# Softmax denominators inverted in PSUM, row maxima dealt over pairs of steps, and five more probability tiles a unit summed on GpSimd

## The chip, the cores and the metric

The kernel runs on one core of one Trainium2 chip. The metric is the device time of one execution in microseconds (us).

## The reference

A transformer block on x of shape (4, 2048, 512): an adaptive layernorm (shift, scale and gate from a small product), causal attention with 16 heads of 32 channels, and a feedforward of the RWKV kind. The change touches the attention alone. All is float32.

```python
scores = jnp.einsum('bqhd,bkhd->bhqk', q, k)
scores = scores + jnp.einsum('bqr,bkr->bqk', q_rope, k_rope)[:, None]
scores = scores / scale
causal = jnp.triu(jnp.ones((Tt, Tt), dtype=bool), k=1)
scores = jnp.where(causal[None, None], -jnp.inf, scores)
w = jax.nn.softmax(scores, axis=-1)
attn = jnp.einsum('bhqk,bkhd->bqhd', w, v).reshape(Bb, Tt, D_MODEL)
return attn @ W_o
```

## The kernel before

The program has three stages: the projection (to about 510 us), the attention (to about 3034 us) and the feedforward. The attention works through 16 units; a unit u is four heads of one batch entry. A unit has four groups j = 0 to 3 of 512 queries each. Group j goes over the 128-key tiles that its queries may see: 4(j+1) steps, 40 in a unit. In the last four steps of a group the diagonal cuts the columns to 512, 384, 256 and 128 (`step_width`), and GpSimd zeroes the triangle with an `affine_select` (L915). FIRST = 0, 4, 12, 24 are the first steps of the groups; here steps are numbered within the unit, and those behind 39 are the next unit's.

What a step t makes on each engine:

- TensorE: for each of four heads two matmuls of scores into one of three banks (L985, L986). In every odd step the output products of steps t-3 and t-2 follow (`weighted_values`, eight instructions a step, into ps_o).
- ScalarE: four exponentials into one of five probability tiles (`probs`, RING = 5, L831).
- The denominators: the sum of the probabilities over all keys. SHARE_OF names the owner of each step. On a "T" step TensorE multiplies the probabilities with ones into ps_d beside the output product. The "G" steps are added by GpSimd into `sum_g` (L934 for the first two, L937 for the others), and one product with ones, the closing (`close_denominators`), brings `sum_g` into ps_d, at step 1 of the next group. Before, group 0 has no G step and no closing.
- VectorE, behind a closing: a copy of ps_d to `rden` (L878), four reciprocals of 128 columns in `rden` (L884), and the product of the output (`o_sb`, which ScalarE copied from ps_o) with `rden` (L888, the normalisation), spread over the two steps behind the closing (`extras`).
- The row maxima: 160 pieces a unit, each a score matmul of 128 queries by up to 512 keys into one of three banks (L971) and a maximum out of the bank on VectorE (L867, or L870 with the mask where the keys are those of the diagonal). A piece is named by its group j and its key chunk kc; those with kc < j are full (512 columns), those with kc = j are 128, 256, 384 or 512 wide. When a group's pieces are done, TensorE transposes the maxima (the "turn", L959), VectorE negates them (L861), and a DMA puts them into a row of the score operand. PLAN says between which score matmuls the pieces stand, for work that is due up to 30 steps later. TensorE and VectorE take the pieces in one order, and TensorE may be three pieces ahead.

The order on each engine is written out in full by the program; nothing is rearranged when it runs. `denominators_ready`, `den_taken` and `o_ready` are semaphores between TensorE and VectorE, `cleared` and `sum_added` come from GpSimd. The output product of a step waits for `cleared` when the step is one of the last four of its group.

Of the kernel before, what the change touches and what calls it, by code (L numbers as in the profile page):

```python
# [22 lines left out]
P = 128  # L23
# [521 lines left out]
SHARE_OF = ("TTTT", "GGGGTGGG", "GGGTGGGGTGGG", "GGGTGGGTGGGGTGGG")  # L545
# [8 lines left out]
def sum_shares():  # L554

    out = []
    for j, owners in enumerate(SHARE_OF):
        mine = [i for i, o in enumerate(owners) if o == "G"]
        if mine:
            out += [(j, (mine[0], mine[1]))] + [(j, (i,)) for i in mine[2:]]  # L560
    return out
# [7 lines left out]
def room(s):  # L569

    if s == NSTEP:
        return CH // 2
    return step_width(s) * (2 if any(s - FIRST[j] in (2, 3) for j in range(1, TCH)) else 5) // 5


def maximum_plan():

    plan = {t: [] for t in range(NU * NSTEP)}
    early = lambda it: it[-1] == 0
    spans = []  # L580
    for u in range(NU):
        mine = [[(u, *it) for it in max_pieces(j)] for j in range(TCH)]
        if u == 0:
            spans += [(u, mine[1], range(0, 3)), (u, mine[2], range(3, 11)), (u, mine[3], range(11, 22))]
        else:
            spans += [(u - 1, mine[0] + [it for it in mine[2] if early(it)] + mine[1], range(23, NSTEP + 1)),
                      (u, [it for it in mine[2] if not early(it)] + mine[3], range(2, 22))]
    for u, items, steps in spans:
        seen, done = 0, 0
        for s in steps:  # L590
            seen += room(s)
            upto = len(items) * seen // sum(map(room, steps))
            plan[NSTEP * u + s] += items[done:upto]
            done = upto
# [52 lines left out]
def attention(nc, keep, scratch, ops):  # L647


    with ExitStack() as ctx:  # L650
# [15 lines left out]
        rden, *o_sb = (sb(n, [P, CH], F32) for n in ("rden", "o_sb0", "o_sb1"))  # L666
# [13 lines left out]
        den_ready = sem("den_ready")  # L680
        den_taken, rden_ready = sem("den_taken"), sem("rden_ready")
# [21 lines left out]
        SHARES = sum_shares()  # L703
# [9 lines left out]
        def summed(u, j, i):  # L713

            return len(SHARES) * (u + 1) + next(n for n, (jj, steps) in enumerate(SHARES) if jj == j and i in steps) + 1

        CLOSED = [j for j in range(TCH) if set(SHARE_OF[j]) != {"T"}]

        def denominators_ready(u, j):

            if j not in CLOSED:
                return pv_done, NSTEP * u + FIRST[j] + STEPS[j] + RING
            return den_ready, len(CLOSED) * u + CLOSED.index(j) + 2
# [811 lines left out]
```

## Time and profile before

| | us |
|---|---|
| three runs | 3919.67 median (3917.86 to 3922.95) |
| the profiled execution | 3919.98 |
| its span in the trace | 3918.3 |
| TensorE busy | 3643.2 (93%) |
| VectorE busy | 2844.3 (73%) |
| GpSimd busy | 2444.0 (62%) |
| ScalarE busy | 1805.1 (46%) |

Busy times are sums of instruction times over the span. The end of a matmul is modelled, so two matmuls in a row overlap; the distance from one start to the next is the time that one takes in the stream. A wait is the idle time of an engine, put down to the instruction that ended it.

### The profile page before, as it was taken

Reading aid. Unit: us, or ns where it says so; the run is one execution under the profiler, and the core shown is the slowest. Engines: PE = TensorE matmul, PEld = TensorE weight load, DVE = VectorE, ACT = ScalarE, POOL = GpSimd, SP = SyncE. Lnnn points to the kernel's source line nnn. Section 1 sums busy time; section 2 is a strip of 40 time slices with the busy share of each in tenths; the row PEclk is TensorE's granted clock in tenths of the full one; section 3 lists DMA queues with packets and bytes.
Section 4 is the critical chain, followed back from the end, with each engine's and each line's share of the span. In section 5 each row is a group of like instructions: output and inputs, shape, how many; then the busy total and the mean of one; then the engine's idle time right before and its main releaser. Section 6 shows DMA issues by size and latency. Waiting matters only on the chain. (4 is left out here: it accounts for less than half of the span.)

```text
span 3918.3 us, 56697 instructions
## 1 busy us (share of the span) xinstructions
PE 3643.2 (93%) x19808; PEld 2454.7 (63%) x19808; DVE 2844.3 (73%) x5454; ACT 1805.1 (46%) x3401; POOL 2444.0 (62%) x1145
## 2 busy tenths in 40 slices
PE   7999879999999999999999999999998699999998
PEld 3777645665665665656656666566564577777776
DVE  5777577777777777778777777777773577777776
ACT  2343335555555555555555555555554233333332
POOL 1333237677777787777777867777778355555555
PEclk8999989999999999999999999999999799999999
DMA  5789743463543634634436345344430311111110
GB/s 176 258 270 296 264 99 76 90 134 78 113 98 83 141 79 95 135 73 108 104 88 130 79 103 127 76 106 109 90 83 6 129 64 54 64 57 53 61 64 32
DMA packets 232267, 425.83 MB, mean 109 GB/s; under 512 B 25332, under 2 KB 26868, under 8 KB 231928
## 3 DMA queue, kind: packets, MB, share of 16 engines
q1 hardware_dynamic: 231992, 423.10, 41.5%
q8 instruction: 121, 1.98, 0.2%
q14 instruction: 90, 0.74, 0.1%
q10 hardware_dynamic: 64, 0.02, 0.0%
HBM read 300.86 MB, written 121.65 MB: 108 GB/s over the span
## 5 line engine op out<-in xcount | busy, mean ns | idle before, releaser
L831 ACT ACTIVATE att_probs<-att_ps_s 128x512 f32<-128x512 f32 (+3 forms) x2560 | 1316.4, 534 | 1153.9 <-PE att_ps_s L986 1058.3
L937 POOL TENSOR_TENSOR att_sum_g<-att_sum_g,att_probs 128x2048 f32<-128x2048 f32 (+3 forms) x384 | 1447.3, 3769 | 207.3 <-ACT att_probs L831 171.6
L867 DVE TENSOR_REDUCE att_piece_max<-att_ps_m 128x1 f32<-128x512 f32 x1536 | 973.1, 680 | 218.6 <-PE att_ps_m L971 215.6
L985 PE MATMUL att_ps_s<-att_q_a,att_k_a 128*128 128x512 f32 (+3 forms) x2560 | 962.2, 380 | 15.8 <-DMA att_q_b<-att_neg_max 15.7
L986 PE MATMUL att_ps_s<-att_q_b,att_k_b 65*128 65x512 f32 (+3 forms) x2560 | 942.5, 371 | 0.0
L971 PE MATMUL att_ps_m<-att_k_a,att_q_a 128*128 128x512 f32 (+3 forms) x1840 | 674.3, 391 | 72.6 <-DVE att_piece_max L867 36.1
L870 DVE CUSTOM_DVE_ANT_0 att_ps_m<-att_ps_m,mask_qk 128x128 f32<-128x128 f32 (+3 forms) x1024 | 489.5, 507 | 291.4 <-PE att_ps_m L971 281.0
L985 PEld LDWEIGHTS att_ps_s<-att_q_a,att_k_a 128*128 128x128 f32 x2560 | 491.5, 192 | 137.1 <-issue 61.6
L971 PEld LDWEIGHTS att_ps_m<-att_k_a,att_q_a 128*128 128x128 f32 x1840 | 348.2, 192 | 350.1 <-DVE att_piece_max L867 129.1
L992 PE MATMUL att_ps_o<-att_probs,att_v 128*32 128x512 f32 (+3 forms) x5120 | 549.4, 535 | 7.3 <-POOL att_probs L915 7.3
L986 PEld LDWEIGHTS att_ps_s<-att_q_b,att_k_b 65*128 65x128 f32 x2560 | 489.2, 191 | 68.0
L934 POOL TENSOR_TENSOR att_sum_g<-att_probs 128x2048 f32<-128x2048 f32 x48 | 221.3, 4610 | 389.5 <-PE att_ps_d L992 217.6
L971 PE MATMUL att_ps_m<-att_k_next,att_q_a 128*128 128x128 f32 (+1 forms) x720 | 275.9, 390 | 32.2 <-DVE att_piece_max L870 32.2
L992 PEld LDWEIGHTS att_ps_o<-att_probs,att_v 128*32 128x32 f32 x5120 | 133.5, 109 | 250.7 <-issue 162.9
L915 POOL TENSOR_SCALAR_AFFINE_SELECT att_probs<-att_probs 128x512 f32<-128x512 f32 x256 | 161.6, 634 | 114.7 <-ACT att_probs L831 114.7
L884 DVE RECIPROCAL att_rden<-att_rden 128x128 f32<-128x128 f32 x256 | 232.5, 930 | 0.1
L971 PEld LDWEIGHTS att_ps_m<-att_k_next,att_q_a 128*128 128x128 f32 x720 | 140.5, 195 | 120.8 <-issue 47.1
L1379 POOL TENSOR_TENSOR ffn_x_kept<-ffn_x_kept,ffn_gate_r 128x512 f32<-128x512 f32 x64 | 101.6, 1588 | 163.6 <-DVE ffn_gate_r L1256 163.6
L1172 DVE TENSOR_TENSOR ffn_x<-ffn_ps_ffn,ffn_gate 128x512 f32<-128x512 f32 x64 | 44.3, 692 | 169.8 <-PE ffn_ps_ffn L61 142.5
L1322 ACT ACTIVATE ffn_act_f<-ffn_relu 128x512 f32<-128x512 f32 x64 | 40.4, 632 | 257.1 <-DVE ffn_relu L1251 256.2
L888 DVE TENSOR_TENSOR att_o_sb<-att_o_sb,att_rden 128x512 f32<-128x512 f32 x64 | 153.5, 2399 | 1.1
L59 PE MATMUL ffn_ps_ffn<-ffn_w_o_hi,ffn_att_hi 128*128 128x512 f32 x256 | 108.5, 424 | 43.9 <-ACT ffn_gate_r L1316 38.5
(173 smaller groups left out, 5230.1 us busy)
## 6 DMA issues: line engine op xcount, KB each, us to landing
att_q_a<-s_q_hi SPq DMA_DIRECT2D x128, 256.0 KB, 6.4
att_q_a<-s_qr_hi SPq DMA_DIRECT2D x128, 256.0 KB, 7.2
prj_x_sb<-in_x_dram SPq DMA_DIRECT2D x16, 1024.0 KB, 5.4
s_q_hi<-prj_q_hi SPq DMA_DIRECT2D x16, 1024.0 KB, 4.4
s_q_lo<-prj_q_lo SPq DMA_DIRECT2D x16, 1024.0 KB, 6.5
s_k_hi<-prj_k_hi SPq DMA_DIRECT2D x16, 1024.0 KB, 4.5
s_k_lo<-prj_k_lo SPq DMA_DIRECT2D x16, 1024.0 KB, 6.5
s_v<-prj_v_sb SPq DMA_DIRECT2D x16, 1024.0 KB, 9.4
```

The lines of the kernel that those rows point to most:

```text
L831: act.activation(probs[t % RING][:, hh, c0:CH], ps_s[(GH * t + hh) % SBANKS][:, c0:CH], ACT.Exp, scale=SCALE).then_inc(probs_ready, 1)
L867: dve.tensor_reduce(top, ps_m[:, bank, :], AX_X, ALU.max).then_inc(piece_taken, 1)
L870: dve.tensor_tensor_reduce(ps_m[:, bank, 0:width], ps_m[:, bank, 0:width], keep["mask_qk"][:, CH - width:CH], 1.0, MASKED, ALU.add, ALU.ma ...
L884: dve.reciprocal(cols, cols).then_inc(rden_ready, 1)
L888: dve.tensor_tensor(o_sb[j % 2][:], o_sb[j % 2][:], rden[:], ALU.mult).then_inc(o_ready, 1)
L915: pool.affine_select(out=at, in_=at, compare_op=ALU.is_ge, fill=0.0, base=0, pattern=[[0, GH], [1, P]], channel_multiplier=-1).then_inc(cl ...
L934: pool.tensor_tensor(sum_g[:], probs[(FIRST[j] + steps[0]) % RING][:], new, ALU.add).then_inc(sum_added, 1)
L937: pool.tensor_tensor(sum_g[:, :, c0:CH], sum_g[:, :, c0:CH], new, ALU.add).then_inc(sum_added, 1)
L971: mm(ps_m[:, bank, 0:width], q_a[j][:, hh, r * P:(r + 1) * P], keys, start=True, stop=True).then_inc(piece_ready, 1)
L985: mm(out[:, c0:CH], k_a[:, hh, i * P:(i + 1) * P], q_a[j][:, hh, c0:CH], start=True, stop=False)
L986: last = mm(out[:, c0:CH], k_b[:, hh, i * P:(i + 1) * P], q_b[j][:, hh, c0:CH], start=False, stop=True)
L992: last = mm(out[hh * HD:(hh + 1) * HD, c0:CH], stat(hh), mov[:, hh, c0:CH], start=start, stop=stop, skip_group_check=True)
```

## The change

The reciprocals are taken in ps_d, in place, and the normalisation reads ps_d; `rden` and its copy are gone. So ps_d is free for the next group only when the normalisation is done: where TensorE waited for `den_taken` it waits for `o_ready`.

SHARE_OF gives GpSimd 35 steps a unit where it had 30, and TensorE five where it had ten. Group 0 is now summed by GpSimd in its first two steps: a copy of 128 columns of each head and an addition of 384 (`head`), and so it has a closing as well, in step 5, ahead of the output products of steps 2 and 3, whose T products come behind it. On GpSimd the head stands between the clearing of steps 0 and 1 and that of steps 2 and 3, and it waits for the closing of the group before (`closed`). Group 1 has no T step left: its closing opens ps_d.

The plan of the maxima is new: `deal` hands them out over pairs of steps. A pair gets as many as make the ratio of VectorE's work to TensorE's the same in every pair, with 2.8 for a piece and 19 for the denominators of a group that fall into the pair. The order of the groups' pieces changes too, and pieces are dealt from step 24 of the unit before to step 21.

```diff
--- before.py
+++ after.py
@@ -542,7 +542,7 @@
 
 
 LAG = 2
-SHARE_OF = ("TTTT", "GGGGTGGG", "GGGTGGGGTGGG", "GGGTGGGTGGGGTGGG")
+SHARE_OF = ("GGTT", "GGGGGGGG", "GGGGGGGGTGGG", "GGGGGGTGGGGGTGGG")
 
 
 def step_width(s):
@@ -551,47 +551,71 @@
     return CH - max(0, s - FIRST[j] - TB * j) * P
 
 
-def sum_shares():
-
-    out = []
+def sums_made():
+
+    made, read_by = [], {}
     for j, owners in enumerate(SHARE_OF):
         mine = [i for i, o in enumerate(owners) if o == "G"]
-        if mine:
-            out += [(j, (mine[0], mine[1]))] + [(j, (i,)) for i in mine[2:]]
+        if j == 0:
+            made.append((j, "head"))
+        for n, i in enumerate(mine):
+            if n:
+                made.append((j, i))
+            read_by[j, i] = len(made) + (n == 0)
+    return made, read_by
+
+
+def max_pieces(j):
+
+    return [(j, hh, r, kc) for kc in range(j + 1) for hh in range(GH) for r in range(TB)]
+
+
+def streams(m):
+
+    own = sum(2 * GH * step_width(s) for s in (2 * m, 2 * m + 1))
+    due = [(2 * m - 2) % NSTEP, (2 * m - 1) % NSTEP]
+    for s in due:
+        j = max(j for j in range(TCH) if FIRST[j] <= s)
+        own += GH * step_width(s) * (2 if SHARE_OF[j][s - FIRST[j]] == "T" else 1)
+    return own / CH + GH * any(FIRST[j] == (2 * m) % NSTEP for j in range(TCH))
+
+
+PIECE, CLOSING = 2.8, 19
+
+
+def deal(items, pairs):
+
+    closes = lambda m: CLOSING * any(FIRST[j] + 2 == 2 * m for j in range(TCH))
+    share = lambda rho, m: max(0.0, (rho * streams(m) - closes(m)) / (PIECE - rho))
+    low, high = 0.0, PIECE - 0.01
+    for _ in range(60):
+        rho = (low + high) / 2
+        low, high = (rho, high) if sum(share(rho, m % (NSTEP // 2)) for m in pairs) < len(items) else (low, rho)
+    out, seen = {}, 0.0
+    for m in pairs:
+        for half in (0, 1):
+            done = round(seen)
+            seen += share(high, m % (NSTEP // 2)) / 2
+            out[2 * m + half] = items[done:round(seen)]
+    assert sum(map(len, out.values())) == len(items)
     return out
 
 
...
 def maximum_plan():
 
-    plan = {t: [] for t in range(NU * NSTEP)}
...
+    half = NSTEP // 2
     for u in range(NU):
...
+        part = {(j, kc): [(u, *it) for it in max_pieces(j) if it[-1] == kc] for j in range(TCH) for kc in range(j + 1)}
         if u == 0:
...
+            spans = [(part[1, 0] + part[1, 1], range(0, 1)), (part[2, 0] + part[2, 1] + part[2, 2], range(2, 5)),
+                     (sum((part[3, kc] for kc in range(TCH)), []), range(5, 11))]
         else:
...
+            order = ((0, 0), (1, 0), (2, 0), (1, 1), (2, 1), (2, 2), (3, 0), (3, 1), (3, 2), (3, 3))
+            spans = [(sum((part[p] for p in order), []), range(half * u - half + 12, half * u + 11))]
+        for items, pairs in spans:
+            for t, some in deal(items, pairs).items():
+                plan[t] += some
...
-        rden, *o_sb = (sb(n, [P, CH], F32) for n in ("rden", "o_sb0", "o_sb1"))
+        o_sb = [sb(n, [P, CH], F32) for n in ("o_sb0", "o_sb1")]
...
@@ -700,7 +724,7 @@
 
...
-        SHARES = sum_shares()
+        MADE, READ_BY = sums_made()
 
         def heads_ready(u, s, hh):
 
@@ -712,15 +736,13 @@
 
         def summed(u, j, i):
 
-            return len(SHARES) * (u + 1) + next(n for n, (jj, steps) in enumerate(SHARES) if jj == j and i in steps) + 1
-
-        CLOSED = [j for j in range(TCH) if set(SHARE_OF[j]) != {"T"}]
+            return len(MADE) * (u + 1) + READ_BY[j, i]
 
         def denominators_ready(u, j):
 
-            if j not in CLOSED:
+            if j == 0:
                 return pv_done, NSTEP * u + FIRST[j] + STEPS[j] + RING
-            return den_ready, len(CLOSED) * u + CLOSED.index(j) + 2
+            return closed, TCH * u + j + 2
 
 
         STEP_OF = [(u, j, i) for u in range(NU) for j in range(TCH) for i in range(STEPS[j])]
@@ -850,7 +872,6 @@
         def _(dve):
             dve.sem_inc(o_ready, 1)
             dve.sem_inc(rden_ready, TB)
-            dve.sem_inc(den_taken, 1)
 
             def maxima(items):
 
@@ -873,23 +894,18 @@
                         dve.wait_ge(piece_taken, seq + 1)
                         dve.tensor_reduce(row_max[:, j, :], piece_max[:, j, :, 0:j + 1], AX_X, ALU.max).then_inc(max_ready, 1)
 
-            def take_denominators(u, j):
-                waits(dve, denominators_ready(u, j), (o_ready, TCH * u + j + 1))
-                dve.tensor_copy(rden[:], ps_d[:]).then_inc(den_taken, 1)
-
             def invert(u, j, r):
                 if r == 0:
-                    dve.wait_ge(den_taken, TCH * u + j + 2)
-                cols = rden[:, r * P:(r + 1) * P]
+                    dve.wait_ge(*denominators_ready(u, j))
+                cols = ps_d[:, r * P:(r + 1) * P]
                 dve.reciprocal(cols, cols).then_inc(rden_ready, 1)
 
             def normalise(u, j):
                 waits(dve, (rden_ready, TB * (TCH * u + j + 2)), (o_copied, TCH * u + j + 2))
-                dve.tensor_tensor(o_sb[j % 2][:], o_sb[j % 2][:], rden[:], ALU.mult).then_inc(o_ready, 1)
+                dve.tensor_tensor(o_sb[j % 2][:], o_sb[j % 2][:], ps_d[:], ALU.mult).then_inc(o_ready, 1)
 
             extras = {t: [] for t in range(NU * NSTEP + LAG + 2)}
             for t, (u, j) in CLOSE_AT.items():
-                extras[t + 1].append(lambda u=u, j=j: take_denominators(u, j))
                 for r in range(TB):
                     extras[t + 1 + r // 2].append(lambda u=u, j=j, r=r: invert(u, j, r))
                 extras[t + 2].append(lambda u=u, j=j: normalise(u, j))
@@ -903,11 +919,9 @@
 
         @block.gpsimd
         def _(pool):
-            pool.sem_inc(sum_added, len(SHARES))
-            pool.sem_inc(den_ready, 1)
+            pool.sem_inc(sum_added, len(MADE))
+            pool.sem_inc(closed, 1)
             pool.memset(as_f32(k_b[2 * HD:2 * HD + 1, :, :]), 1.0).then_inc(ones_ready, 1)
-
-            shares = {(j, steps[-1]): steps for j, steps in SHARES}
 
             def clear_future(u, j, i):
 
@@ -921,18 +935,24 @@
                         s = FIRST[j] + i
                         c0 = CH - step_width(s)
                         new = probs[s % RING][:, :, c0:CH]
-                        steps = shares.get((j, i), ())
-                        if i < TB * j and steps:
+                        mine = [n for n, o in enumerate(SHARE_OF[j]) if o == "G"]
+                        makes = i in mine[1:]
+                        if i < TB * j and makes:
                             pool.wait_ge(probs_ready, heads_ready(u, s, GH - 1))
                         if i >= TB * j:
                             wait_alone(pool, probs_ready, heads_ready(u, s, GH - 1), pool_mark)
                             clear_future(u, j, i)
-                            if steps:
+                            if makes:
                                 pool.wait_ge(cleared, future_cleared(u, j, i))
-                        if len(steps) == 2:
-                            pool.wait_ge(den_ready, len(CLOSED) * u + CLOSED.index(j) + 1)
-                            pool.tensor_tensor(sum_g[:], probs[(FIRST[j] + steps[0]) % RING][:], new, ALU.add).then_inc(sum_added, 1)
-                        elif steps:
+                        if not makes:
+                            continue
+                        if i == mine[1]:
+                            first = probs[(FIRST[j] + mine[0]) % RING]
+                            pool.wait_ge(closed, TCH * u + j + 1)
+                            if c0:
+                                pool.tensor_copy(sum_g[:, :, 0:c0], first[:, :, 0:c0]).then_inc(sum_added, 1)
+                            pool.tensor_tensor(sum_g[:, :, c0:CH], first[:, :, c0:CH], new, ALU.add).then_inc(sum_added, 1)
+                        else:
                             pool.wait_ge(sum_added, summed(u, j, i) - 1)
                             pool.tensor_tensor(sum_g[:, :, c0:CH], sum_g[:, :, c0:CH], new, ALU.add).then_inc(sum_added, 1)
 
@@ -1010,25 +1030,28 @@
                 last = over_keys(ps_o, lambda hh: v[:, i // TB, i % TB, hh * HD:(hh + 1) * HD], probs[s % RING],
                                  start=(i == 0), stop=(i == STEPS[j] - 1), c0=c0)
                 if SHARE_OF[j][i] == "T":
-                    first = i == SHARE_OF[j].index("T")
+                    first = j > 0 and i == SHARE_OF[j].index("T")
                     if first:
-                        pe.wait_ge(den_taken, TCH * u + j + 1)
-                    last = over_keys(ps_d, ones, probs[s % RING], start=first,
-                                     stop=(j not in CLOSED and i == STEPS[j] - 1), c0=c0)
+                        pe.wait_ge(o_ready, TCH * u + j + 1)
+                    last = over_keys(ps_d, ones, probs[s % RING], start=first, stop=(j == 0 and i == STEPS[j] - 1), c0=c0)
                 last.then_inc(pv_done, 1)
 
             def close_denominators(u, j):
-                if "T" not in SHARE_OF[j]:
-                    pe.wait_ge(den_taken, TCH * u + j + 1)
+                opens = j == 0 or "T" not in SHARE_OF[j]
+                if opens:
+                    pe.wait_ge(o_ready, TCH * u + j + 1)
                 pe.wait_ge(sum_added, summed(u, j, SHARE_OF[j].rindex("G")))
-                last = over_keys(ps_d, ones, sum_g, start=("T" not in SHARE_OF[j]), stop=True)
-                last.then_inc(den_ready, 1)
+                last = over_keys(ps_d, ones, sum_g, start=opens, stop=(j > 0))
+                last.then_inc(closed, 1)
 
             for item in AHEAD:
                 maximum(item)
             pe.wait_ge(ones_ready, 1)
             for t in range(NU * NSTEP + LAG):
                 parts = [lambda hh=hh: scores(*STEP_OF[t], hh) for hh in range(GH) if t < NU * NSTEP]
+                closing = CLOSE_AT.get(t)
+                if closing and closing[1] == 0:
+                    parts.append(lambda: close_denominators(*closing))
                 if t > LAG and t % 2 == 1:
                     parts.append(lambda: [weighted_values(*STEP_OF[due]) for due in (t - LAG - 1, t - LAG)])
                 items = PLAN.get(t, [])
@@ -1036,8 +1059,8 @@
                     part()
                     for it in items[len(items) * n // len(parts):len(items) * (n + 1) // len(parts)]:
                         maximum(it)
-                if t in CLOSE_AT and CLOSE_AT[t][1] in CLOSED:
-                    close_denominators(*CLOSE_AT[t])
+                if closing and closing[1] > 0:
+                    close_denominators(*closing)
 
 
 def feedforward(nc, keep, dram, scratch, out):
```

## Rows read from the trace of the kernel before

**Rows 1.** Waits of TensorE in the attention, 541 to 3034 us.
```profile
PE att_ps_m L971 <- DVE att_piece_max L870: 51.7, 35, 2.2
PE att_ps_m L971 <- DVE att_piece_max L867: 35.7, 18, 4.2
```
**Rows 2.** Timeline of TensorE: start, length, instruction, [idle before it <- releaser].
```profile
912.39 0.50 PE L971 MATMUL att_ps_m<-att_k_a,att_q_a 128*128 128x512 f32 x1 [1.93 <-DVE att_piece_max L867]
...
1222.24 0.50 PE L971 MATMUL att_ps_m<-att_k_a,att_q_a 128*128 128x512 f32 x1 [1.96 <-DVE att_piece_max L867]
...
1272.32 0.50 PE L971 MATMUL att_ps_m<-att_k_next,att_q_a 128*128 128x512 f32 x1 [2.13 <-DVE att_piece_max L870]
...
1347.68 0.39 PE L971 MATMUL att_ps_m<-att_k_a,att_q_a 128*128 128x256 f32 x1 [1.26 <-DVE att_piece_max L870]
...
2937.84 0.50 PE L971 MATMUL att_ps_m<-att_k_a,att_q_a 128*128 128x512 f32 x1 [1.93 <-DVE att_piece_max L867]
```
**Rows 3.** Windows, PE alone: us, PE busy, PE clock granted, DMA share, GB/s.
```profile
1220.00:1230.00 10.00, 8.04 (x35) 0.83 0.08 28
```
**Rows 4.** Timeline of VectorE, two normalisations.
```profile
1219.14 2.45 DVE L888 TENSOR_TENSOR att_o_sb<-att_o_sb,att_rden 128x512 f32<-128x512 f32 x1
...
1267.85 4.14 DVE L888 TENSOR_TENSOR att_o_sb<-att_o_sb,att_rden 128x512 f32<-128x512 f32 x1
```
**Rows 5.** Timeline of GpSimd, the additions that ran at those times.
```profile
1216.46 4.57 POOL L937 TENSOR_TENSOR att_sum_g<-att_sum_g,att_probs 128x2048 f32<-128x2048 f32 x1
...
1266.89 4.54 POOL L937 TENSOR_TENSOR att_sum_g<-att_sum_g,att_probs 128x2048 f32<-128x2048 f32 x1
```
**Rows 6.** Tile att_rden, whole run: lengths in ns min/median/max, first and last start.
```profile
L884 DVE RECIPROCAL att_rden<-att_rden x256: 893/937/954, 545.2 to 3032.7; 128x128 f32<-128x128 f32 x128
L878 DVE COPY att_rden<-att_ps_d x64: 682/692/692, 544.0 to 3029.5; 128x512 f32<-128x512 f32 x64
L888 DVE TENSOR_TENSOR att_o_sb<-att_o_sb,att_rden x64: 691/2394/4660, 550.8 to 3033.6; 128x512 f32<-128x512 f32 x64
```
**Rows 7.** Tile ffn_ps_ffn, VectorE alone, 3100 to 3900 us.
```profile
L1172 DVE TENSOR_TENSOR ffn_x<-ffn_ps_ffn,ffn_gate x60: 691/692/693, 3114.0 to 3848.7; 128x512 f32<-128x512 f32 x60
```
**Rows 8.** Timeline of TensorE: four closings in a row, and one output product.
```profile
1322.17 1.06 PE L992 MATMUL att_ps_d<-att_sum_g,ones 128*32 128x512 f32 x8
...
1336.64 0.64 PE L992 MATMUL att_ps_o<-att_probs,att_v 128*32 128x256 f32 x8
...
1368.46 1.07 PE L992 MATMUL att_ps_d<-att_sum_g,ones 128*32 128x512 f32 x8
...
1416.95 1.06 PE L992 MATMUL att_ps_d<-att_sum_g,ones 128*32 128x512 f32 x8
...
1476.73 1.06 PE L992 MATMUL att_ps_d<-att_sum_g,ones 128*32 128x512 f32 x8
```
**Rows 9.** Timeline of TensorE: two scores, and the output products of two steps.
```profile
1208.22 0.40 PE L985 MATMUL att_ps_s<-att_q_a,att_k_a 128*128 128x512 f32 x1
1208.45 0.40 PE L986 MATMUL att_ps_s<-att_q_b,att_k_b 65*128 65x512 f32 x1
...
1216.55 1.92 PE L992 MATMUL att_ps_o<-att_probs,att_v 128*32 128x512 f32 x16
1218.40 0.50 PE L971 MATMUL att_ps_m<-att_k_a,att_q_a 128*128 128x512 f32 x1
```
**Rows 10.** Timeline of GpSimd: group 1 of a unit, first and last addition.
```profile
1337.19 4.61 POOL L934 TENSOR_TENSOR att_sum_g<-att_probs 128x2048 f32<-128x2048 f32 x1 [10.00 <-ACT att_probs L831]
...
1360.30 1.29 POOL L937 TENSOR_TENSOR att_sum_g<-att_sum_g,att_probs 128x512 f32<-128x512 f32 x1
```
**Rows 11.** The same in group 3 of the last unit.
```profile
2980.27 37.89 POOL L937 TENSOR_TENSOR att_sum_g<-att_sum_g,att_probs 128x2048 f32<-128x2048 f32 x8
```
**Rows 12.** Groups of instructions by form, 1000 to 2600 us: count | busy, mean ns | idle before.
```profile
L867 DVE TENSOR_REDUCE att_piece_max<-att_ps_m 128x1 f32<-128x512 f32 x977 | 619.6, 680 | 129.9 <-PE att_ps_m L971 127.9
...
L937 POOL TENSOR_TENSOR att_sum_g<-att_sum_g,att_probs 128x1536 f32<-128x1536 f32 x32 | 111.1, 3470 | 2.7
L915 POOL TENSOR_SCALAR_AFFINE_SELECT att_probs<-att_probs 128x512 f32<-128x512 f32 x168 | 106.1, 634 | 58.8 <-ACT att_probs L831 58.8
...
L937 POOL TENSOR_TENSOR att_sum_g<-att_sum_g,att_probs 128x512 f32<-128x512 f32 x31 | 39.9, 1287 | 2.6
```

More of the change, by code:

```diff
@@ L551, in step_width @@
     return CH - max(0, s - FIRST[j] - TB * j) * P
-def sum_shares():
-    out = []
+def sums_made():
+    made, read_by = [], {}
     for j, owners in enumerate(SHARE_OF):
         mine = [i for i, o in enumerate(owners) if o == "G"]
-        if mine:
-            out += [(j, (mine[0], mine[1]))] + [(j, (i,)) for i in mine[2:]]
-    return out
+        if j == 0:
[5 more added lines that the diff above has]
+    return made, read_by
@@ L564, in max_pieces @@
 def max_pieces(j):
     return [(j, hh, r, kc) for kc in range(j + 1) for hh in range(GH) for r in range(TB)]
[L569 to L573, printed above, removed]
+def streams(m):
[5 more added lines that the diff above has]
+    return own / CH + GH * any(FIRST[j] == (2 * m) % NSTEP for j in range(TCH))
@@ new lines @@
+PIECE, CLOSING = 2.8, 19
[13 more added lines that the diff above has]
+    assert sum(map(len, out.values())) == len(items)
+    return out
@@ L576, in maximum_plan @@
 def maximum_plan():
-    plan = {t: [] for t in range(NU * NSTEP)}
-    early = lambda it: it[-1] == 0
-    spans = []
+    plan = {t: [] for t in range(NU * NSTEP + 1)}
+    half = NSTEP // 2
     for u in range(NU):
-        mine = [[(u, *it) for it in max_pieces(j)] for j in range(TCH)]
+        part = {(j, kc): [(u, *it) for it in max_pieces(j) if it[-1] == kc] for j in range(TCH) for kc in range(j + 1)}
         if u == 0:
-            spans += [(u, mine[1], range(0, 3)), (u, mine[2], range(3, 11)), (u, mine[3], range(11, 22))]
-        else:
-            spans += [(u - 1, mine[0] + [it for it in mine[2] if early(it)] + mine[1], range(23, NSTEP + 1)),
-                      (u, [it for it in mine[2] if not early(it)] + mine[3], range(2, 22))]
@@ L588, in maximum_plan @@
[L588 to L594, printed above, removed]
+            spans = [(part[1, 0] + part[1, 1], range(0, 1)), (part[2, 0] + part[2, 1] + part[2, 2], range(2, 5)),
+                     (sum((part[3, kc] for kc in range(TCH)), []), range(5, 11))]
+        else:
+            order = ((0, 0), (1, 0), (2, 0), (1, 1), (2, 1), (2, 2), (3, 0), (3, 1), (3, 2), (3, 3))
+            spans = [(sum((part[p] for p in order), []), range(half * u - half + 12, half * u + 11))]
@@ L679, in attention @@
         o_copied = sem("o_copied")
-        den_ready = sem("den_ready")
-        den_taken, rden_ready = sem("den_taken"), sem("rden_ready")
+        closed = sem("closed")
+        rden_ready = sem("rden_ready")
         kn_in = sem("kn_in")
```

## The prediction

> **What bounds the kernel now.** I read the waits of TensorE first. Between 541 and 3034 us it idles in one place that repeats: in front of a score matmul for the maxima (L971), until VectorE has emptied a bank, 51.7 + 35.7 = 87.4 us in 53 waits [rows 1]. The timeline shows them as three a unit at fixed places, of 1.26, 1.96 and 2.13 us [rows 2]; everywhere else one matmul starts behind the other, 0.23 us apart [rows 9]. So TensorE's stream sets the time, and what a unit takes is its matmuls plus these waits. The first matmul behind the second kind of wait starts at 912.39 us in one unit and at 2937.84 us 13 units later [rows 2]: 155.8 us a unit. Four closings in a row divide a unit: 46.3 us from that of group 3 to that of group 1, 48.5 to that of group 2, 59.8 to the next of group 3 [rows 8]. Some waits also cost clock: in the ten us around the one at 1222 the granted clock is 0.83 [rows 3], so a third of them at 1.2 GHz instead of 2.4, about 1.7 us more. Not every unit has that: the stretches of rows 8 hold none and add up to 154.6, so the clock costs 1.2 us a unit on average.
>
> Why VectorE is late: the normalisation (L888) takes 0.69 to 4.66 us, median 2.39, for one and the same shape [rows 6]. The two of rows 4 end at 1221.59 and 1271.99, each 0.56 us behind the end of the GpSimd addition that ran meanwhile (1221.03 and 1271.43) [rows 4, 5]. It reads two operands in SBUF and waits until GpSimd is through; the maxima are queued behind it on VectorE, and TensorE waits for them once its three banks are full.
>
> **The change, part by part.**
>
> *The normalisation out of PSUM.* It keeps one operand in SBUF. The nearest row is L1172, a product of a PSUM and an SBUF tensor of the same size: 691 to 693 ns in all 60 cases, in a stage where GpSimd works too [rows 7]. I take 0.69 us; the other end is 2.4, no change. The copy of 0.69 us goes as well [rows 6]. Together VectorE is free 2.4 us earlier behind a closing, more than each of the three waits. The Trainium skill, SBUF — State Buffer, "Who interferes with whom", says that a VectorE instruction with two SBUF inputs contends with a GpSimd instruction that reads SBUF, and that one with at most one SBUF input does not. By that rule 0.69 is right; the trace agrees on the first half, and the second is what rows 7 suggest.
>
> *The reciprocals in PSUM.* No row has one there. From SBUF 128 columns take 937 ns [rows 6], far more than reading them can (a reduction reads 512 columns out of PSUM in 680 ns [rows 12]), so I take 0.94, with 0.9 and 2 times that, 1.9, as the ends. The Trainium skill speaks against the change here: VectorE: DVE Perf Modes, "The TRN2 errata", gives a VectorE instruction a fixed 120 cycles with a PSUM source and 58 from SBUF. By that, as an estimate, four reciprocals and the product take 0.3 us more; the copy out of PSUM and the free product out of SBUF in rows 6 show no such difference (0.69 both), and 0.3 us would be hidden. What hides this work is the plan: it deals 0, 1, 2 and 1 pieces to the pairs of steps behind the four closings, and TensorE needs 6 us for such a pair of full steps (16 score matmuls of 0.234 and two output products of 0.925 [rows 9], 5.6, and the pieces) against 4 x 0.94 + 0.69 = 4.45 us on VectorE. In the pair behind group 3's closing (256 and 128 columns) TensorE needs only about 3.7, but the next user of ps_d, the closing of group 0, comes 10 us later (below).
>
> *TensorE's denominators.* A full T step costs 0.925 us, since two steps of output products take 1.85 [rows 9]; one of 384 columns about 0.7. Removed are four full ones (group 0 step 0; group 1; one in group 2; one in group 3) and that of 384 columns: 4.4 us a unit. Added is one closing, 1.0 [rows 8].
>
> *The maxima moved.* A full piece costs TensorE 0.234 us, a masked one by its mean width 0.15 (an estimate from rows 9). Counting `maximum_plan` out, the three stretches have 52, 54 and 54 pieces before (16, 26 and 22 of them masked) and 40, 45 and 75 after (10, 27 and 27 masked). In place of 7 in a full step, which is 4.8 us of VectorE with 0.68 each [rows 12], there are mostly 5 or 6.
>
> *GpSimd.* It gets four full additions more a unit (one each in groups 1, 2 and 3; the fifth step goes into the head) of 37.89 / 8 = 4.74 us [rows 11], and the head: a copy of 512 columns and an addition of 1536. The copy isn't in the trace; 0.63 (one input) and 1.29 (two inputs) bound it, and I take 1.0; with 3.47 [rows 12] the head is 4.5 us. GpSimd cannot start on a group before the group before is closed. So each stretch has a chain of its own: closing (1.0), additions, next closing. TensorE's path is taken from the measured stretch.
>
> Group 0: from group 3's closing to the output product at 1336.64 are 14.5 us before [rows 8]. Less the T products (1.6) and 18 pieces for 12 (2.1), the closing of group 0 starts 10.8 us behind. GpSimd's head and two clearings (1.0 + 4.5 + 1.3) and VectorE's denominators (1.0 + 4.5) both fit, with 4 us over: no wait.
>
> Group 1: GpSimd took 1337.19 to 1361.59, 24.4 us [rows 10]; with one addition more 29.1. The stretch is 10.8 + 1.0 + 29.1 = **40.9**. TensorE alone would need 46.3 - 1.3 (wait) - 0.9 - 0.7 - 0.9 (T) + 1.0 - 2.3 (12 pieces less) = 41.2 at most, and 39.8 if the small waits inside the steps go too (my sum of its matmuls before is 43.6). So GpSimd ends last by about a us here.
>
> Group 2: three full additions more than group 1, 29.1 + 14.2 - 0.3 (a wait in rows 10's stretch) = 43.0, with the closing **44.0**. TensorE: 48.5 - 2.0 - 0.9 - 2.2 = 43.4 at most, 41.7 without small waits. GpSimd ends last again.
>
> Group 3: GpSimd 1.0 + 29.1 + 6 x 4.74 = 58.5. TensorE: 59.8 - 2.1 - 0.9 + 21 pieces more (4.5) = 61.3, and 1.1 for short waits at the dense pairs: **62.4**. TensorE is the bound, and here the change costs 2.6 us.
>
> A unit: 40.9 + 44.0 + 62.4 = 147.3, against 155.8: 8.5 less. That holds for units 1 to 14: 119 us. The first unit has a plan of its own, denser in its first four steps; I give it 3. In the last one there are no pieces behind step 21, and GpSimd bounds group 3 already now (eight additions back to back [rows 11]): -5.4 - 4.5 + 4.7 and the copy at the end -0.7, so 6 less. Sum: 119 + 3 + 6 = 128. The profiled execution took 3919.98, 0.3 above the median of the runs: **3792 us**.
>
> **The rivals.**
> *GpSimd's waits hurt more than they last.* For it: the chains of groups 1 and 2 are the bound by 1 to 2 us, TensorE then waits in front of an output product for `cleared`, and waits of 2 us have cost 1.7 us of clock in about a third of the cases [rows 3]; short waits in the stretches add up on GpSimd's chain too when the probabilities come late. Against: the waits are split in two and are each shorter than 1.96. Two lost clocks and 2 us of wait a unit are 5.4 us, 15 x 5.4 = 80: 3872 at worst, 3835 in the middle.
> *GpSimd keeps up.* If its additions start earlier than I count, TensorE's own 39.8 + 41.7 + 61.3 = 142.8 holds, 4.5 x 15 = 68 less: 3725. Against: the chain starts at a closing, and every link has a row.
> *The normalisation still waits* (2.4 us, not 0.69). Then VectorE needs 6.2 us in pairs of 6; with few pieces there this costs 1 us at three closings, 45 us: 3837.
> *Slower: the reciprocals are slow out of PSUM.* Each closing has about 6 us of cover, 1.3 us for each reciprocal. Beyond, four closings of four reciprocals pay 16 times the excess a unit, since the maxima and ps_d itself wait for them. It eats the 8.5 us at 1.3 + 0.53 = 1.85 us each, twice the row; at 2.5 us the time is 3792 + 15 x 19 = 4080. Against: a length that is 7 ns a column in SBUF is arithmetic and not access.
>
> **How the numbers follow.** The forecast, 3770 to 3815, has 0.50; GpSimd's waits or a late normalisation (3815 to 3872) 0.27; GpSimd keeps up (3725 to 3770) 0.13; a gain under 48 us that is still over 0.2% 0.03; none 0.02; slower 0.05. A measurement here tells 0.2% (8 us) from nothing. Range with two in ten outside: 3750 to 3850. Faster 0.93, same 0.02, slower 0.05.
>
> **What would show it.** Of the changed profile: L888 at 0.69 us throughout; the reciprocals at 0.94; no waits of L971 for VectorE above 1 us; new waits of TensorE for GpSimd in front of the output product of step 21 (about 2 us) and at the closing of group 1 (about 1); distances between closings of 41, 44 and 62; GpSimd without idle time from a closing of group 0 to that of group 2 but for the closings. It is wrong if L971 still waits for VectorE, if a closing waits for `o_ready`, or if the third stretch is shorter than 60.

## The result and the profile after

The changed kernel takes 3798.61 us (median of four runs, 3789.98 to 3807.10) against 3921.22 us for the kernel before (four runs, 3917.86 to 3922.95). The ratio is 0.9691, with a 95% interval from 0.9673 to 0.9708: 3.1% faster, 6.6 us from the 3792 that was predicted. The profiled execution took 3801.18 us, 118.8 less than that of before.

The page's busy times (first section, then the rows of the slices for TensorE and GpSimd):

```profile
PE 3586.7 (94%) x19296; PEld 2423.5 (64%) x19296; DVE 2702.1 (71%) x5390; ACT 1800.5 (47%) x3401; POOL 2722.6 (72%) x1225
...
PE   7999979999999999999999999999996899999998
...
POOL 1333248889889898898898898988986455555555
```

GpSimd is now eight or nine tenths busy throughout the attention; TensorE has 512 instructions fewer. The waits of TensorE in the attention, 541 to 2920 us (total us, times, longest):

```profile
PE att_ps_o L1012 <- POOL att_probs L929: 32.7, 17, 4.2
PE att_ps_d L1012 <- POOL att_sum_g L957: 6.3, 16, 0.9
PE att_ps_s L1005 <- ACT att_probs L853: 4.1, 2, 2.9
PE att_ps_m L991 <- DVE att_piece_max L888: 0.5, 2, 0.3
PE att_ps_m L991 <- DVE att_piece_max L891: 0.3, 1, 0.3
```

The 87.4 us in front of the maxima [rows 1] are down to 0.8. In their place stand two new waits a unit, both for GpSimd. The timeline of TensorE over one unit shows them, with the closings between which the three stretches of a unit are measured:

```profile
1166.95 1.06 PE L1012 MATMUL att_ps_d<-att_sum_g,ones 128*32 128x512 f32 x8 [0.36 <-POOL att_sum_g L957]
...
1201.84 1.21 PE L1012 MATMUL att_ps_o<-att_probs,att_v 128*32 128x512 f32 x8 [1.78 <-POOL att_probs L929]
...
1212.56 1.07 PE L1012 MATMUL att_ps_d<-att_sum_g,ones 128*32 128x512 f32 x8
...
1274.76 1.06 PE L1012 MATMUL att_ps_d<-att_sum_g,ones 128*32 128x512 f32 x8
...
1285.61 1.06 PE L1012 MATMUL att_ps_d<-att_sum_g,ones 128*32 128x512 f32 x8
...
1315.73 1.06 PE L1012 MATMUL att_ps_d<-att_sum_g,ones 128*32 128x512 f32 x8 [0.36 <-POOL att_sum_g L957]
...
1359.79 1.06 PE L1012 MATMUL att_ps_d<-att_sum_g,ones 128*32 128x512 f32 x8
```

These are the closings of groups 1, 2, 3, 0, 1 and 2. From group 3's to group 0's are 10.85 us and on to group 1's 30.12, together 40.97; from group 2's to group 3's 62.20. Group 2's own stretch is 45.61 us in the first of these units and 44.06 in the second. Between the closings of group 3 in the first unit and in the last but one (682.46 and 2762.53 us) lie 14 units of 148.58 us on average.

The tile att_ps_d over the whole run (ns min/median/max) has the reciprocals and the product in their new place:

```profile
L901 DVE RECIPROCAL att_ps_d<-att_ps_d x256: 890/904/967, 542.9 to 2910.9; 128x128 f32<-128x128 f32 x128
L905 DVE TENSOR_TENSOR att_o_sb<-att_o_sb,att_ps_d x64: 670/686/689, 549.7 to 2911.8; 128x512 f32<-128x512 f32 x64
```

### The profile page after: what moved, and what is told of

It reads as the page before. It is cut to its first block and busy times, and to the rows that moved or that the text cites. A ratio compares the mean times of both kernels' runs of the same rounds, so it can differ in the third digit from the quotient of the medians.

```text
span 3799.4 us, 55720 instructions
## 1 busy us (share of the span) xinstructions
PE 3586.7 (94%) x19296; PEld 2423.5 (64%) x19296; DVE 2702.1 (71%) x5390; ACT 1800.5 (47%) x3401; POOL 2722.6 (72%) x1225
## 5 line engine op out<-in xcount | busy, mean ns | idle before, releaser
L957 POOL TENSOR_TENSOR att_sum_g<-att_sum_g,att_probs 128x2048 f32<-128x2048 f32 (+3 forms) x432 | 1665.5, 3855 | 57.3 <-ACT att_probs L853 6.9
L1006 PE MATMUL att_ps_s<-att_q_b,att_k_b 65*128 65x512 f32 (+3 forms) x2560 | 932.2, 368 | 0.0
L991 PE MATMUL att_ps_m<-att_k_a,att_q_a 128*128 128x512 f32 (+3 forms) x1840 | 663.3, 383 | 17.1 <-PEq L215 13.7
L1012 PE MATMUL att_ps_o<-att_probs,att_v 128*32 128x512 f32 (+3 forms) x5120 | 561.3, 546 | 32.7 <-POOL att_probs L929 32.7
L954 POOL TENSOR_TENSOR att_sum_g<-att_probs 128x1536 f32<-128x1536 f32 (+1 forms) x64 | 276.1, 4314 | 173.0 <-PE att_ps_d L1012 173.0
L901 DVE RECIPROCAL att_ps_d<-att_ps_d 128x128 f32<-128x128 f32 x256 | 224.3, 926 | 91.0 <-PE att_ps_d L1012 91.0
L991 PE MATMUL att_ps_m<-att_k_next,att_q_a 128*128 128x128 f32 (+1 forms) x720 | 256.8, 385 | 0.0
L459 POOL TENSOR_TENSOR prj_h_lo<-prj_h_f,prj_h_hi 128x512 fp32r<-128x512 f32 x64 | 80.5, 1292 | 106.4 <-ACT prj_h_hi L404 106.4
L59 PE MATMUL ffn_ps_ffn<-ffn_w_o_hi,ffn_att_hi 128*128 128x512 f32 x256 | 111.6, 436 | 40.9 <-ACT ffn_gate_r L1339 35.4
```

The costliest lines, as they stand in the source:

```text
L59: mm(out, stat[0], mov[0], start=first, stop=False)
L901: dve.reciprocal(cols, cols).then_inc(rden_ready, 1)
L954: pool.tensor_tensor(sum_g[:, :, c0:CH], first[:, :, c0:CH], new, ALU.add).then_inc(sum_added, 1)
L957: pool.tensor_tensor(sum_g[:, :, c0:CH], sum_g[:, :, c0:CH], new, ALU.add).then_inc(sum_added, 1)
L991: mm(ps_m[:, bank, 0:width], q_a[j][:, hh, r * P:(r + 1) * P], keys, start=True, stop=True).then_inc(piece_ready, 1)
L1006: last = mm(out[:, c0:CH], k_b[:, hh, i * P:(i + 1) * P], q_b[j][:, hh, c0:CH], start=False, stop=True)
```

## The experiments

Ten kernels ran. Each was timed in rounds beside the kernel before; the ratio's interval is against that. A median is of four runs, which lie within 3 to 8 us of each other, those of the changed kernel within 17. So a difference of a few us between two medians says little, and one of 10 us little where the changed kernel is one of the two. The column "last closing" is the start of the last closing in the profiled execution; it shows the attention alone. The feedforward behind it is the same program in all, and took 880 to 893 us there. Step owners are written as in SHARE_OF.

| kernel | product, reciprocals | plan | owners | us | ratio | last closing, us |
|---|---|---|---|---|---|---|
| before | SBUF | old | old | 3921 | | 3027.9 |
| psum_only | PSUM | old | old | 3874.1 | 0.985 to 0.992 | 2983.5 |
| plan_only | SBUF | new | old | 3815.2 | 0.971 to 0.975 | 2924.7 |
| psum_plan | PSUM | new | old | 3799.0 | 0.966 to 0.972 | 2907.9 |
| changed | PSUM | new | new | 3798.6 | 0.967 to 0.971 | 2906.4 |
| old_plan | PSUM | old | new | 3811.2 | 0.969 to 0.976 | 2927.2 |
| product_sbuf | product SBUF | new | new | 3832.3 | 0.974 to 0.981 | 2939.7 |
| head_only | PSUM | new | new in group 0 | 3778.8 | 0.962 to 0.966 | 2890.9 |
| t_group2 | PSUM | new | one T back in group 2 | 3763.4 | 0.958 to 0.962 | 2875.7 |
| t_moved | PSUM | new | T of group 2 one earlier | 3768.3 | 0.959 to 0.963 | 2883.5 |
| t_group12 | PSUM | new | a T back in groups 1 and 2 | 3765.8 | 0.959 to 0.963 | 2882.1 |
| t_group2_last | PSUM | new | t_group2, and the end | 3754.0 | 0.956 to 0.960 | 2864.2 |

**psum_only.** The old plan and the old owners, with the edit of the change to `invert` and `normalise`:

```diff
-                cols = rden[:, r * P:(r + 1) * P]
+                cols = ps_d[:, r * P:(r + 1) * P]
...
-                dve.tensor_tensor(o_sb[j % 2][:], o_sb[j % 2][:], rden[:], ALU.mult).then_inc(o_ready, 1)
+                dve.tensor_tensor(o_sb[j % 2][:], o_sb[j % 2][:], ps_d[:], ALU.mult).then_inc(o_ready, 1)
...
-                        pe.wait_ge(den_taken, TCH * u + j + 1)
+                        pe.wait_ge(o_ready, TCH * u + j + 1)
```

> The kernel before with one part of the change: reciprocals in ps_d, product read from ps_d, TensorE waits for o_ready; old owners of the steps, old plan of the maxima. Theory 1 (the product in SBUF waits for GpSimd and so makes the three waits of L971 a unit): L888 takes 0.69 us, the three waits of 1.3, 2.0 and 2.1 us go with their clock, 6.5 us a unit less; but the first T product of group 0 comes some 3 us behind the closing of group 3 and now waits for the whole inversion (4.5 us and the pieces between), 3 us a unit more. Net 3.5 us a unit, about 3865 us. Rival (the pieces dealt right behind a closing make VectorE late, wherever the product reads): waits of L971 above 1 us stay at the same places, 3900 us or more.

3874 us, 9 above the expectation. The three waits of L971 are gone, and the one for the inversion has come, at the length that was expected. TensorE's waits, 541 to 3000 us, and one of them in the timeline:

```profile
PE att_ps_d L986 <- DVE att_o_sb L883: 46.1, 15, 3.1
```
```profile
1305.64 1.94 PE L986 MATMUL att_ps_d<-att_probs,ones 128*32 128x512 f32 x8 [3.08 <-DVE att_o_sb L883]
```

So the product in SBUF made the three waits: the copy of 0.69 us [rows 6] went too, but each wait was longer than that. The longer hold on ps_d gives about half of the gain back.

**psum_plan.** psum_only, with `room` and the old `maximum_plan` replaced by the change's `streams`, `deal` and `maximum_plan`.

> As the run before, and with the new plan of the maxima; the owners of the steps are the old ones (30 for GpSimd, 10 for TensorE). Theory 1: TensorE's matmuls are 3.4 us a unit more than in the changed kernel, GpSimd is never the bound, and no clock is lost in group 2; group 0's first T product waits for the inversion about 2.5 us. About 149.5 us a unit, 3815 us. Rival (the plan brings nothing beside the product in PSUM): same time as the run before.

3799 us, 16 below the expectation and equal to the changed kernel. The wait for the inversion is 0.7 us, since no maxima are dealt ahead of it. In one unit the stretches between closings are 42.7, 43.6 and 63.0 (closings at 1131.32, 1173.97, 1217.53 and 1280.53 us), and the granted clock is full from 600 to 2780 us. The five steps that the change then gives to GpSimd bring nothing: the last closings, 2907.9 and 2906.4 us, say the same as the medians.

**plan_only.** The kernel before with that plan alone.

> The kernel before with the new plan of the maxima alone; product and reciprocals in SBUF, old owners. Theory 1 (product in SBUF waits for GpSimd): with 0 to 2 pieces dealt behind a closing most of the lateness is hidden, but waits of L971 of 1 to 2 us stay where the product takes 4 us: about 3850 us. Rival (the plan alone took the waits): 3800 us, as with the product in PSUM.

3815 us: my theory missed by 35 us and the rival is nearer. The product still has both operands in SBUF, but now it seldom meets a GpSimd addition: this is the tile att_o_sb of plan_only, of the whole run, against a median of 2394 in [rows 6].

```profile
L908 DVE TENSOR_TENSOR att_o_sb<-att_o_sb,att_rden x64: 691/909/3843, 551.7 to 2930.8; 128x512 f32<-128x512 f32 x64
```

The timelines of VectorE and of GpSimd in plan_only say why:

```profile
1188.59 1.14 DVE L908 TENSOR_TENSOR att_o_sb<-att_o_sb,att_rden 128x512 f32<-128x512 f32 x1
...
1232.93 0.69 DVE L908 TENSOR_TENSOR att_o_sb<-att_o_sb,att_rden 128x512 f32<-128x512 f32 x1
```
```profile
1184.56 4.62 POOL L954 TENSOR_TENSOR att_sum_g<-att_probs 128x2048 f32<-128x2048 f32 x1 [7.26 <-PE att_ps_d L1012]
1189.32 23.83 POOL L957 TENSOR_TENSOR att_sum_g<-att_sum_g,att_probs 128x2048 f32<-128x2048 f32 x5
...
1228.39 4.62 POOL L954 TENSOR_TENSOR att_sum_g<-att_probs 128x2048 f32<-128x2048 f32 x1 [5.51 <-PE att_ps_d L1012]
1233.15 19.17 POOL L957 TENSOR_TENSOR att_sum_g<-att_sum_g,att_probs 128x2048 f32<-128x2048 f32 x4
```

GpSimd's first addition behind a closing (1184.56, 1228.39 us) and VectorE's inversion start together. With no piece or one between, VectorE comes to the product as that first addition ends and before the second begins. In the kernel before there were five pieces between closing and product in one of the two places of [rows 4] and two in the other, and the product came within the second addition. One wait of 0.95 us a unit is left, behind group 0. The new plan both deals by pairs of steps and orders the groups anew; which of the two does it was not tested.

**old_plan.** The changed kernel with the old plan.

> The changed kernel with the old plan of the maxima. If the plan is what took the waits away: waits of L971 for VectorE of 1 us and more come back behind the closings of groups 1 and 2, about 3850 us. If the product in PSUM did it: stretches of 42.8 (TensorE), 44.7 (TensorE) and 58.3 us (GpSimd, since the old plan has 21 pieces fewer in group 3), 146 to 148 us a unit against 148.6: within 30 us of the changed kernel, 3770 to 3815 us.

3811 us, 13 above the changed kernel: the second branch. By the last closings it is 21 us above. One wait for VectorE of 1.20 us a unit is there, 8.6 us behind the closing of group 3. The stretch to group 3's closing is 58.28 us in a unit (58.22 to 58.29 in all but the last), which is GpSimd's chain, forecast as 58.3. The two other stretches were forecast 42.8 and 44.7 and came out 45.3 and 45.9 in most units, so a unit takes 149.4 us and not 146 to 148. The closing of group 3 in two units running:

```profile
1135.46 1.06 PE L992 MATMUL att_ps_d<-att_sum_g,ones 128*32 128x512 f32 x8 [0.71 <-POOL att_sum_g L937]
...
1284.86 1.07 PE L992 MATMUL att_ps_d<-att_sum_g,ones 128*32 128x512 f32 x8 [0.71 <-POOL att_sum_g L937]
```

So the plan and PSUM are two cures for one trouble: with the old owners PSUM alone takes 47 us off, the plan alone 106, both together 122.

**product_sbuf.** The changed kernel with a copy back to SBUF ahead of the product:

```diff
+                dve.tensor_copy(rden[:], ps_d[:]).then_inc(rden_copied, 1)
+                dve.wait_ge(rden_copied, TCH * u + j + 1)
-                dve.tensor_tensor(o_sb[j % 2][:], o_sb[j % 2][:], ps_d[:], ALU.mult).then_inc(o_ready, 1)
+                dve.tensor_tensor(o_sb[j % 2][:], o_sb[j % 2][:], rden[:], ALU.mult).then_inc(o_ready, 1)
```

> The changed kernel, but the inverted denominators are copied from ps_d to SBUF and the product reads them there: two SBUF operands again, and one copy of 0.69 us more. Theory 1: the product again takes 0.7 to 4.7 us, median above 2.5 since GpSimd is busier; VectorE needs some 7.5 us in a pair of steps that gives 6: waits of L971 behind the closings of groups 1, 2 and 0, of 1 to 2 us in group 3's stretch, and the GpSimd-bound stretches move less: 3810 to 3840 us. Rival (the new plan alone leaves room enough): no wait of L971 above 0.5 us, 3799 us as before.

3832 us, as expected: 34 us more. The product takes 0.69 to 4.56 us, but its median is 1.74, where above 2.5 was expected. At 1194.04 us the product runs 4.56 us, and TensorE then waits 2.34 us:

```profile
1194.04 4.56 DVE L907 TENSOR_TENSOR att_o_sb<-att_o_sb,att_rden 128x512 f32<-128x512 f32 x1
```
```profile
1193.47 9.53 POOL L959 TENSOR_TENSOR att_sum_g<-att_sum_g,att_probs 128x2048 f32<-128x2048 f32 x2
```
```profile
1199.25 0.50 PE L993 MATMUL att_ps_m<-att_k_a,att_q_a 128*128 128x512 f32 x1 [2.34 <-DVE att_piece_max L888]
```

So with GpSimd this busy the new plan alone does not keep a product with two operands in SBUF clear of the additions. Part of that is the place of the copy: GpSimd's second addition starts at 1193.47 us, and without the copy of 0.69 us the product would have started at about 1193.3, just before it.

**t_group2.**

```diff
-SHARE_OF = ("GGTT", "GGGGGGGG", "GGGGGGGGTGGG", "GGGGGGTGGGGGTGGG")
+SHARE_OF = ("GGTT", "GGGGGGGG", "GGGGTGGGTGGG", "GGGGGGTGGGGGTGGG")
```

> The changed kernel with one step of group 2 (its fifth) back on TensorE: GpSimd 34 steps a unit, TensorE 6. Theory 1 (in group 2 GpSimd's chain is the bound, and its wait costs clock too): GpSimd's chain is 4.7 us shorter, TensorE's 0.9 longer; the wait of 1.75 us before the output product of step 20 and the lost clock go, group 2's stretch falls from 45.3 (mean) to 42.7 us, 2.6 us a unit, about 3760 us. Rival (an added product on TensorE costs what it costs, since TensorE is 94% busy): 0.9 us a unit more, 3813 us.

3763 us. TensorE does more and the kernel is 35 us faster. Its waits, 541 to 2860 us, and its window from 600 to 2780 (us, busy, granted clock, DMA share, GB/s):

```profile
PE att_ps_o L1012 <- POOL att_probs L929: 4.4, 15, 0.3
```
```profile
600.00:2780.00 2180.00, 2171.87 (x13173) 1.00 0.49 108
```

Group 2's stretch is 43.65 us, 1.0 above the 42.7 expected; group 3's fell from 62.25 to 61.76. `deal` reads SHARE_OF, so the edit moves a piece from group 3 to group 2 as well, and the 35 us are of both. By the last closings it is 31 us.

**t_moved.** As t_group2, but with `"GGGGGGGTGGGG"` for group 2, so the same number of additions as the change.

> The changed kernel with TensorE's step of group 2 one place earlier (step 7 of the group instead of step 8), the same number of additions. The clearing that the output product of step 20 waits for comes 4.7 us earlier, but GpSimd's chain to the closing is as long. Theory 1 (the chain sets the stretch at 44.1 us, the wait in front of the output product only adds the clock): wait moves to the closing, 44.1 us if no clock is lost there, up to 18 us less than the changed kernel, 3780 to 3800 us. Rival (the wait for the clearing is the whole trouble): group 2's stretch falls to 42 us, 50 us less, 3750 us.

3768 us, some 12 below the expected range. Group 2's stretch is 43.97 to 44.06 us in units 2 to 15, as the chain says, and 46.17 in unit 1, behind a wait of 1.74 us for a DMA. The wait for GpSimd now lies at the closing and just ahead of it, in two parts under 0.5 us, and the clock holds behind it until the last unit. Over units 1 to 14 this gives group 2 some 17 us, within the 18 expected. What the expectation lacked is group 3, 61.7 instead of 62.2 us, 7 us more. The timeline of TensorE in t_moved at the closing of group 2:

```profile
1208.60 0.43 PE L1012 MATMUL att_ps_o<-att_probs,att_v 128*32 128x128 f32 x8 [0.42 <-POOL att_probs L929]
1209.96 1.06 PE L1012 MATMUL att_ps_d<-att_sum_g,ones 128*32 128x512 f32 x8 [0.44 <-POOL att_sum_g L957]
```

**head_only.** SHARE_OF = ("GGTT", "GGGGTGGG", "GGGTGGGGTGGG", "GGGTGGGTGGGGTGGG").

> The changed kernel with the old owners in groups 1, 2 and 3: of GpSimd's five more steps only the head of group 0 is left (with its closing). Against psum_plan (3799 us, all old owners) TensorE has 0.65 us a unit less work and no wait for o_ready (0.7 us): theory 1 says 1.4 us a unit less, 3779 us; the sum of the four other steps is then worth minus 20 us as changed, and 16 us if one of them stays on TensorE. Rival (the head costs what it saves, as GpSimd's clearings stand behind it): 3799 us.

3778.8 us, as expected. The expectation counts wrongly: the head takes two of the five steps, so three are left, one in each of groups 1, 2 and 3. The head and its closing save 20 us (17 by the last closings); the other three steps cost 20 as changed (16). With TensorE keeping two steps in group 2 (t_group2) the other two save 15, by either measure.

**t_group12.** As t_group2, with `"GGGGTGGG"` for group 1.

> As t_group2 (3763 us), and the fifth step of group 1 back on TensorE too: GpSimd 33 steps, TensorE 7. GpSimd's chain in group 1 (30.1 us from closing to closing) falls to 25.4, TensorE's path there grows by 0.9 from somewhere between 28.9 and 30.1. Theory 1 (both engines end together in group 1 now): within 0.9 us a unit, 3758 to 3775 us, so nothing is to be had there. Rival (GpSimd's chain hides a TensorE path much shorter than it): faster than 3750 us.

3766 us, not told apart from t_group2 (3763) by the medians; by the last closings it is 6 us later, and a unit takes 146.83 us against 146.46. In group 1 the two engines end within half a us of each other.

**t_group2_last.** As t_group2, with an owner list of its own for group 3 of the last unit:

```diff
+LAST_SHARE = "GGGTGGTGGTGTTGGG"
+
+
+def share_of(u, j):
+    return LAST_SHARE if (u, j) == (NU - 1, TCH - 1) else SHARE_OF[j]
```

> As the run before, and group 3 of the last unit gets three more steps on TensorE (5 of 16), since no maxima are left there and GpSimd's additions stand back to back. Theory 1: that stretch falls from 57.9 us to about 47, so 10 us under the run before, about 3749 us. Rival (the end is bound by something else): same as the run before.

3754 us, 9.4 less than t_group2; the last stretch is 46.86 us (closings at 2817.33 and 2864.19), forecast 47. This is the fastest version, 1.2% under the changed kernel and 4.2% under the one before.

## Why the prediction was right

It was right in the time and in the mechanism; one cost was priced too low, and the nearness of 3799 to 3792 is in part luck. By the closings, of before [rows 8] and after, means of units 1 to 14:

| | predicted | measured |
|---|---|---|
| groups 0 and 1, with the closings | 40.9 | 40.96 |
| group 2 | 44.0 | 45.37 (44.06 to 44.10 in four units) |
| group 3 | 62.4 | 62.25 |
| a unit | 147.3 | 148.58 |
| units 1 to 14, saved | 119 | 104.2 |
| first unit, saved | 3 | 13.1 |
| last unit, saved | 6 | 4.2 |
| outside the attention | 0 | -2.7 |

The last four measured terms add up to the 118.8 us between the profiled executions, where 128 was predicted. The units before took 156.0 us between the same closings, not 155.8.

*The normalisation* takes 0.69 us as taken, and the reciprocals 0.90, not slower than from SBUF (0.94). That settles the slower rival, and the Trainium skill's fixed cost (VectorE: DVE Perf Modes, "The TRN2 errata") does not show here: by it, as an estimate, each reciprocal would be 65 ns longer out of PSUM, and the median is 33 ns shorter. That row of the Trainium skill is for a result in SBUF, and the reciprocals write to PSUM; but the product does write to SBUF, and its median of 686 ns out of PSUM is no longer than the 691 of a free one out of SBUF [rows 6]. The other rule of the Trainium skill (SBUF — State Buffer, "Who interferes with whom") holds in both halves: with GpSimd adding almost all the time, 64 products with one operand in SBUF took at most 0.689 us, and in product_sbuf they took up to 4.56.

*GpSimd's chain* is the bound of group 1, and of group 2 where the clock holds. In the timeline it runs with no gap above 0.15 us from 1168.18 to 1210.93 us, 42.75, predicted 43.0:

```profile
1168.18 4.60 POOL L954 TENSOR_TENSOR att_sum_g<-att_probs 128x2048 f32<-128x2048 f32 x1 [1.38 <-PE att_ps_d L1012]
1172.92 28.28 POOL L957 TENSOR_TENSOR att_sum_g<-att_sum_g,att_probs 128x2048 f32<-128x2048 f32 x6
1201.15 1.22 POOL L929 TENSOR_SCALAR_AFFINE_SELECT att_probs<-att_probs 128x512 f32<-128x512 f32 x2
...
1209.64 1.29 POOL L957 TENSOR_TENSOR att_sum_g<-att_sum_g,att_probs 128x512 f32<-128x512 f32 x1
```

The two new waits stand where the prediction put them: 1.74 to 1.78 us for the clearing of step 20, which is queued behind the addition of step 19 (predicted "step 21", about 2 us), and 0.36 at the closing of group 1 (predicted about 1).

*What was mis-sized* is the cost of the wait in group 2. The forecast took that stretch as GpSimd's chain and gave the clock nothing; the first rival said that the wait costs clock as well, and that came in part. In 10 of the 14 units the clock fell to 1.2 GHz at the end of the wait or just behind it, and TensorE then came to the closing after GpSimd; windows of TensorE around two of them (us, busy, granted clock, DMA share, GB/s):

```profile
1790.00:1800.00 10.00, 8.26 (x50) 0.83 0.69 153
2240.00:2250.00 10.00, 8.88 (x41) 0.66 0.73 160
```

That is 45.37 - 44.06 = 1.3 us a unit, 18 us. t_moved is the test: with the wait in two short parts the clock held and the stretch was the chain. The first unit gave 13 us instead of 3, since its waits before were longer than those of the others (4.21, 1.89 and 2.14 us for VectorE and 2.40 for a DMA), and made up for 10 us of the miss. Nothing in the forecast foresaw that.

Two smaller things in the working do not hold. GpSimd gets three full additions more a unit, one each in groups 1, 2 and 3, and not four; the sums use three. And the 1.1 us "for short waits at the dense pairs" of group 3 came as time but not as waits: TensorE is idle for 0.1 us in that stretch. Between psum_only and psum_plan the 21 pieces more cost 5.7 us there (57.3 to 63.0), where 4.5 was counted, so a piece costs 0.27 us on average.

*What the prediction did not see* is how its savings combine. The whole was right, but not what each part is worth. GpSimd's five steps take 3.4 us a unit from TensorE; beside psum_plan (148.97 us a unit between the same closings) the changed kernel's 148.58 gains 0.4. Up to group 1's closing it is 1.7 us shorter and in group 3 0.7, and in group 2 it is some 2 longer, by the wait and the clock. Nor did the prediction see that the new plan alone would end most of the waits: I took 2.4 us as the product's price wherever it stood, while the plan moves it in between two additions at two of its places. plan_only, 106 us faster than before, was what showed it.

## What to carry to other kernels

When work moves from the engine that sets the time to another, add up the other engine's chain between the points where both must meet, stretch by stretch: GpSimd was 72% busy over the run, but from one closing to the next it worked without a pause in two of the four groups here, and one step moved back, with the plan that follows from it, was worth 35 us. A two-operand VectorE instruction in SBUF next to a busy GpSimd cost up to 4 us more here, the rest of GpSimd's instruction, and the engine behind paid it; put one operand in PSUM, or keep queued work away from behind it. Price a wait of TensorE with the clock that may fall behind it, not by its length.

## What the runs showed of the hardware

- The clock does not fall behind every wait, and length alone does not decide it. Behind the wait of 1.75 us in the changed kernel the lower level came in 10 of 14 units, behind those of 1.93 to 2.17 us in the kernel before in 11 of 29, behind those of 2.34 us (product_sbuf) and 3.07 us (psum_only) in 14 of 15 each. Behind those of 0.70 us (psum_plan), 0.95 us (plan_only) and 1.20 us (old_plan), 15 of each, it never came. Why the same wait costs clock in one unit and not in the next was not tested.
- A GpSimd copy of 128x512 took 611 ns (16 times, all alike), less than half of an addition of that size with two operands [rows 12].
- A reciprocal in PSUM, in place, takes what it takes in SBUF: 904 ns against 937 for 128 columns.
